# Expert layers with the weight chunks stationary and the tokens moving, and the expert blocks written out

## What is computed

```
logits = t_norm @ router_w + router_b          # 8 experts, the two best taken, weights normalised
gate = x @ gate_w[e] + gate_b[e]               # 256 -> 512
up   = x @ up_w[e] + up_b[e]                   # 256 -> 512
h    = silu(gate) * up
y    = h @ down_w[e] + down_b[e]               # 512 -> 256
t    = t + sum over the two experts of weight * y
```

## Time and profile before

| | us |
|---|---|
| median of 3 runs | 454.25 (454.06 to 455.29) |
| span of the profiled execution | 453.7 |
| first token transposes of the expert blocks to the end of the span | 243.1 to 453.7 |
| busy: PE / DVE / ACT / POOL | 346.5 / 343.3 / 209.2 / 288.8 |
| mean granted TensorE clock | 0.851 |

### The profile page before, as it was taken

One profiled execution on the slowest core, in us unless ns is written; L12 is line 12 of the kernel. 1 busy time (PEld: TensorE's weight loads), 2 busy tenths in 40 slices (PEclk: granted clock), 3 DMA queues, 4 the chain that ended last, 5 costly groups with the idle time before them and its releaser, 6 DMA issues.

```text
span 453.7 us, 13159 instructions
## 1 busy us (share of the span) xinstructions
PE 346.5 (76%) x4491; PEld 214.4 (47%) x4492; DVE 343.3 (76%) x693; ACT 209.2 (46%) x343; POOL 288.8 (64%) x459
## 2 busy tenths in 40 slices
PE   0078677767866766697259998999999999999971
PEld 0077434444444454542023654656566566565540
DVE  6988799799899999877882776666776776677650
ACT  1047637755956857645501433334434434433430
POOL 5616456666666666644585367777877878788651
PEclk9997568668668668689569999999999999999995
DMA  8410002322322222507764132333233333323322
GB/s 197 123 36 1 2 2 96 95 94 97 95 92 92 92 95 94 144 2 194 219 248 139 25 48 46 48 56 58 46 56 55 51 49 55 58 46 58 56 25 23
DMA packets 24960, 35.27 MB, mean 78 GB/s; under 512 B 4992, under 2 KB 18304, under 8 KB 24160
## 3 DMA queue, kind: packets, MB, share of 16 engines
q1 hardware_dynamic: 16256, 24.46, 17.5%
q0 software_dynamic: 7488, 10.23, 14.1%
q10 hardware_dynamic: 1184, 0.14, 0.2%
HBM read 25.39 MB, written 9.44 MB: 77 GB/s over the span
## 4 chain that ended last, share of the span: by engine, by line
PE 25%; DVE 23%; issue 19%; POOL 13%; DMA 9%; ACT 5%; DVEq 2%; POOLq 1%; SPq 1%; ACTq 0%
PE bank L881 6%; DMA w_stage<-token_rows,q_hi 5%; POOL w_stage L513 4%; PE bank L902 3%; POOL small L509 3%; DVE att L1348 2%; PE bank L549 2%; DVE s_exp L1314 2%; DVE v_exp L1367 2%; PE bank L777 2%; DVE q_exp L1382 2%; POOL v_exp L488 2%; PE bank L664 2%; DVE maxes L1307 2%; DMA token_rows<-z_stack 1%
## 5 line engine op out<-in xcount | busy, mean ns | idle before, releaser
L881 PE MATMUL bank<-w_exp,w_stage 128*128 x468 | 113.7, 380 | 1.3 <-issue 0.2
L526 POOL DMA_INDIRECT out_dram<-w_stage,q_hi x39 | 62.4, 1600 | 16.9 <-issue 16.9
L881 PEld LDWEIGHTS bank<-w_exp,w_stage 128*128 128x128 f16 x468 | 45.6, 97 | 41.8 <-issue 4.6
L408 POOL TENSOR_TENSOR w_exp<-w_stage,w_exp 128x1024 f16<-128x1024 f32 (+1 forms) x24 | 51.0, 2129 | 22.4 <-ACT w_exp L1041 22.4
L902 PE MATMUL bank<-w_exp,q_exp 128*128 x468 | 58.6, 276 | 2.1 <-DVE q_exp L1587 2.1
L513 POOL DMA_INDIRECT w_stage<-token_rows,q_hi x39 | 48.1, 1234 | 6.0 <-issue 6.0
L1570 DVE TENSOR_TENSOR v_exp<-bank,x_rows 128x512 f32<-128x512 f32 x39 | 27.0, 692 | 32.9 <-PE bank L881 32.8
L1146 ACT ACTIVATE w_stage<-w_stage,gate 128x256 f32<-128x256 f32 x39 | 19.8, 508 | 68.2 <-DVE w_stage L1592 68.2
L902 PEld LDWEIGHTS bank<-w_exp,q_exp 128*128 128x128 f16 x468 | 43.0, 98 | 11.8 <-issue 5.4
L1127 ACT ACTIVATE w_stage<-bank 128x256 f16<-128x256 f32 x39 | 14.9, 383 | 52.9 <-PE bank L869 52.9
L1587 DVE TENSOR_TENSOR q_exp<-bank,q_exp 128x512 f16<-128x512 f32 x39 | 27.0, 692 | 10.2 <-ACT q_exp L1138 10.0
(11 more groups left out here) (253 smaller groups left out, 814.2 us busy)
## 6 DMA issues: line engine op xcount, KB each, us to landing
w_stage<-in_L_ffn_gate_w_dram SPq DMA_DIRECT2D x8, 512.0 KB, 3.5
w_stage<-in_L_ffn_up_w_dram SPq DMA_DIRECT2D x8, 512.0 KB, 3.5
w_stage<-in_L_ffn_down_w_dram SPq DMA_DIRECT2D x8, 512.0 KB, 3.5
x_rows<-in_x_dram SPq DMA_DIRECT2D x8, 256.0 KB, 6.1
out_dram<-x_rows SPq DMA_DIRECT2D x4, 512.0 KB, 6.0
token_rows<-z_stack SPq DMA_DIRECT2D x4, 512.0 KB, 6.0
x_rows<-in_L_ffn_gate_b_dram SPq DMA_DIRECT2D x1, 2048.0 KB, 11.6
z_stack<-in_L_ffn_up_b_dram SPq DMA_DIRECT2D x2, 1024.0 KB, 6.8
```

The source lines that it names most:

```text
L408: pool.tensor_tensor(lo, w_stage[:, k, :], hi, ALU.subtract).then_inc(s["w_lo_done"], 1)
L526: pool.indirect_dma_start(out, bass.IndirectOffsetOnAxis(s_idx[par], 0), yw[par], None, compute_op=ALU.add).then_inc(s["y_scattered"], 16)
L881: mm = pe.matmul(GU[par][k][:], xs[par][:, c, :], w_exp[:, w * W_EXP + k * W_PIECE + c * FF:][:, bass.ds(e, FF)], start=(n == 0), stop=(n ...
```

## The change

- `hidden` turns its operands round: a 128x128 chunk of the weights is stationary and the 128 tokens move. For each of gate and up there are four chunks f of the 512 FF units, two halves c of the features and three parts: 24 pairs of a weight load and a matmul of 128 columns where there were six of 512. The result has **FF units on partitions**, which is what `down` needs as stationary operand, so `hidden_turned` is gone.
- With FF units on partitions a bias is a column. `gate_b` and `up_b` are loaded once as 64 rows of 128 (`b_rows`), turned by one PE transpose in `fold_vectors` and copied to `b_cols` by DVE. ACT's `silu` reads the gate's PSUM bank and adds the bias itself, in four chunks; DVE's `gated` adds the up bias and multiplies in one instruction a chunk, four a block. The 4 MB of broadcast bias loads and the two bias additions go.
- PE's order is now hidden(b+1, gate), hidden(b+1, up), tokens_in(b+2), down(b). On DVE a block is down_bias(b-1), gated(b+1), tokens_low(b+2), hidden_low(b+1).
- `gather` and `scatter` take the index column of the table directly, without copy; one hold instruction is left, in `scatter`. Gather b+3 stands ahead of scatter b, as in the loop before. The two `xg` buffers stay.
- The loops over blocks are written out in Python on all engines, so block numbers are constants; the expert's number stays in a register.

```diff
@@
-BODY = (BLOCKS - 3) // 4
+FF_CHUNKS = FF // P
...
+        b_cols = sb("b_cols", [P, 2 * EXPERTS * FF // P])
+        b_rows = att_n[0:64, 1, 0:P]
-        gate_b_all = x_rows[:].rearrange("p n l -> p (n l)")
-        up_b_all = xn.rearrange("p n l -> p (n l)")
...
@@ SyncE
+            for i, b in enumerate((gate_b, up_b)):
+                rows = slice(EXPERTS * FF // P * i, EXPERTS * FF // P * (i + 1))
+                sp.dma_start(b_rows[rows, :], b.rearrange("e (f p) -> (e f) p", p=P)).then_inc(s["r_in"], 16)
...
-            sp.wait_ge(s["rt_ps"], 2 * (TILES // 4))
-            sp.dma_start(gate_b_all, gate_b.rearrange("e i -> (e i)").partition_broadcast(P)).then_inc(s["bias_rows"], 16)
...
-                sp.dma_start(up_b_all[:, half], up_rows[half].partition_broadcast(P)).then_inc(s["up_rows"], 16)
@@ GpSimd
-                pool.tensor_copy(g_idx[par], t_gather[:, bass.ds(b, 1)]).then_inc(s["gcol_ready"], 1)
...
+            def gather(b):
+
+                if b >= 2:
                     pool.wait_ge(s["xt_ps"], b - 1)
...
+                pool.indirect_dma_start(xg[b % 2], None, token_rows,
+                                        bass.IndirectOffsetOnAxis(t_gather[:, b:b + 1], 0))\
+                    .then_inc(s[f"x_got{b % 2}"], 16)
+
+            def scatter(b):
+
+                pool.wait_ge(s["y_ready"], b + 1)
+                if b >= 1:
                     pool.wait_ge(s["y_scattered"], 16 * b)
...
+                pool.tensor_tensor(hold[b], one_word, one_word, ALU.mult)
+                pool.indirect_dma_start(out, bass.IndirectOffsetOnAxis(t_scatter[:, b:b + 1], 0), yw[b % 2], None,
...
+            for b in range(3):
+                gather(b)
+            for b in range(BLOCKS):
+                if b + 3 < BLOCKS:
+                    gather(b + 3)
+                scatter(b)
@@ TensorE
-                pe.wait_ge(s["r_in"], 32)
+                pe.wait_ge(s["r_in"], 64)
+                pe.transpose(bank[7][:, 256:256 + 2 * EXPERTS * FF // P], b_rows, ident[0:64, 0:64])
...
+            def hidden(b, k, e):
 
                 if k == 0:
                     pe.wait_ge(s["xl_ready"], b + 1)
...
+                if b >= 2:
+                    pe.wait_ge(s["silu_ready"] if k == 0 else s["h_ready"], FF_CHUNKS * (b - 1))
+                for f in range(FF_CHUNKS):
                     for c in range(2):
...
+                        for xs, w in ((x_hi, 0), (x_lo, 0), (x_hi, 1)):
+                            mm = pe.matmul(GU[b % 2][k][:, P * f:P * f + P],
+                                           w_exp[:, w * W_EXP + k * W_PIECE + c * FF + P * f:][:, bass.ds(e, P)],
+                                           xs[b % 2][:, c, :], start=(c == 0 and xs is x_hi and w == 0),
+                                           stop=(c == 1 and w == 1))
+                mm.then_inc(s["gate_ps"] if k == 0 else s["up_ps"], 1)
...
-                    mm = pe.transpose(HT[:, P * c:P * c + P], h_sb[par][:, P * c:P * c + P], ident[:])
...
+            for b in range(BLOCKS):
+                if b + 1 < BLOCKS:
+                    e = weights_of(b + 1)
+                    hidden(b + 1, 0, e)
+                    hidden(b + 1, 1, e)
+                e = weights_of(b)
+                if b + 2 < BLOCKS:
+                    load_expert(b + 2)
+                    tokens_in(b + 2)
+                down(b, e)
@@ ScalarE
+            def silu(b):
+                e = act.value_load(t_expert[0:1, b:b + 1], min_val=0, max_val=EXPERTS - 1)
...
+                act.wait_ge(s["gate_ps"], b + 1)
+                for f in range(FF_CHUNKS):
+                    act.activation(g_silu[b % 2][:, P * f:P * f + P], bank[2 * (b % 2)][:, P * f:P * f + P], ACT.Silu,
+                                   bias=b_cols[:, bass.ds(e * FF_CHUNKS + f, 1)]).then_inc(s["silu_ready"], 1)
...
+            for b in range(BLOCKS):
+                if b >= 1:
+                    weigh(b - 1)
+                if b + 1 < BLOCKS:
+                    silu(b + 1)
+                if b + 2 < BLOCKS:
+                    tokens_high(b + 2)
+                if b + 1 < BLOCKS:
+                    hidden_high(b + 1)
+            weigh(BLOCKS - 1)
@@ VectorE
+                    step(dve.tensor_copy(b_cols[:], bank[7][:, 256:256 + 2 * EXPERTS * FF // P]))
...
+            def gated(b):
+                e = expert_of(b)
...
+                dve.wait_ge(s["up_ps"], b + 1)
+                for f in range(FF_CHUNKS):
+                    cols = slice(P * f, P * f + P)
+                    dve.wait_ge(s["silu_ready"], FF_CHUNKS * b + f + 1)
+                    dve.scalar_tensor_tensor(
+                        out=h_sb[b % 2][:, cols], in0=bank[2 * (b % 2) + 1][:, cols],
+                        scalar=b_cols[:, bass.ds(e * FF_CHUNKS + EXPERTS * FF_CHUNKS + f, 1)],
+                        in1=g_silu[b % 2][:, cols], op0=ALU.add, op1=ALU.mult).then_inc(s["h_ready"], 1)
...
+            for b in range(BLOCKS):
+                if b >= 1:
+                    down_bias(b - 1)
+                if b + 1 < BLOCKS:
+                    gated(b + 1)
+                if b + 2 < BLOCKS:
+                    tokens_low(b + 2)
+                if b + 1 < BLOCKS:
+                    hidden_low(b + 1)
+            down_bias(BLOCKS - 1)
```

More of the change, by code:

```diff
@@ L496, in _ @@
             pool.wait_ge(s["pad_out"], 16)
[L500 to L505, removed]
+            hold = [ga_flat[0:1, 256 + i:257 + i] for i in range(BLOCKS)]
+            one_word = t_weight[0:1, 0:1]
+            def gather(b):
+                if b >= 2:
                     pool.wait_ge(s["xt_ps"], b - 1)
-                    pool.wait_ge(s[f"x_got{par}"], 16 * turn)
-                    pool.wait_ge(s["gcol_ready"], b)
-                    pool.tensor_tensor(hold[0], one_word, one_word, ALU.mult)
-                pool.tensor_copy(g_idx[par], t_gather[:, bass.ds(b, 1)]).then_inc(s["gcol_ready"], 1)
[L511 to L514, removed]
@@ L896, in down @@
+            def down(b, e):
                 pe.wait_ge(s["hl_ready"], b + 1)
-                if not first:
+                if b >= 1:
                     pe.wait_ge(s["yadd_ready"], b)
                 n = 0
-                for c in range(4):
+                for c in range(FF_CHUNKS):
                     for hs, w in ((h_hi, 0), (h_lo, 0), (h_hi, 1)):
-                        mm = pe.matmul(YB[:, 0:L_COL], hs[par][:, c, :],
+                        mm = pe.matmul(YB[:, 0:L_COL], hs[b % 2][:, c, :],
@@ L1608, in _ @@
-            tokens_low(0, 0)
-            tokens_low(1, 1)
-            e0 = expert_of(0)
-            dve.wait_ge(s["bias_rows"], 32)
-            gate_bias(0, 0, e0, first=True)
-            dve.wait_ge(s["up_rows"], 32)
-            up_bias(0, 0, e0)
-            gated(0, 0, first=True)
-            dve_block(0, 0, first=True)
-            with dve.Fori(0, BODY) as i:
-                for k in range(4):
-                    dve_block(4 * i + k + 1, (k + 1) % 2)
-            dve_block(BLOCKS - 2, 1, more=1)
@@ L1621, in _ @@
-            dve_block(BLOCKS - 1, 0, more=0)
+            tokens_low(0)
+            gated(0)
+            tokens_low(1)
+            hidden_low(0)
+            dve.wait_ge(s["bias_rows"], 16)
+            for b in range(BLOCKS):
+                if b >= 1:
+                    down_bias(b - 1)
[5 more added lines that the diff above has]
+                    hidden_low(b + 1)
```

211 lines of the change are left out of this document (53 added, 158 removed).

## The result

| | before | after |
|---|---|---|
| median | 454.22 us (454.06 to 455.29, 4 runs) | 506.26 us (505.67 to 506.65, 4 runs) |
| span of the profiled execution | 453.7 | 504.6 |
| ratio of the runs | | 1.115 (95% interval 1.112 to 1.118) |
| mean granted TensorE clock | 0.851 | 0.867 |

A forecast was written before the change was run, and what follows sets the result against it. PE's register steps, in a loop closing through DVE, were to bound each block: up(1) ends at 255.05, plus 37 periods of 6.05 us, 17.25 of tail, 0.25 for the bias copy and 0.55 around the span: 497.0 us, range 484 to 524.

The forecast's parts named there:

- 0.125 us a step: PE's queue: each register-addressed weight slice costs a 0.125 us step; gate and up's 32 take 4.0 us a block.
- A loop that closes through DVE: From up's end through hand-off, four DVE chunks, tokens_low and PE's 31 further steps: 6.05 us a block against 4.94.
- The overlap beside it: PE's queue: register load, token transposes and down's 8 steps, 1.5 us, fit into the 1.95 us PE waits.
- the hand-off does not close: Rival: DVE's chunks don't delay the tokens, PE's queue alone needs 5.6 us a block, 480 us; chance 0.04.
- Beside the loop and buy nothing: Removed hidden transposes (0.43 us of PE), bias additions and old product (2.1 us of DVE) gain nothing.
- "nothing" for GpSimd: Dropping index copies and three of four hold instructions on GpSimd was priced at nothing.
- The floor of 4.4 us for the scatters: GpSimd: each scatter waits for the previous landing; 3.8 us, 0.18 hold and some 0.4 issue give 4.4 us.
- The clock: Rival: PE's clock falls to 1.2 GHz, a block takes 7.3 us; 521 us with half the blocks; chance 0.18.
- Not the bound: Rival: in gate and up an idle PE is fed every 0.057 us, block 4.85 us, 450.2 us; chance 0.06.
- dearer loads: Rival: every register-addressed weight load costs a step, 48 instead of 32, block 8.05 us, 571 us; chance 0.05.
- the first rival: Gate and up steps stay but PE's queue feeds pairs every 0.057 us, 450.2 us; chance 0.06.
- The start: Before the blocks: copying the turned bias on DVE adds 0.25 us; 0.55 us lies around the profiled span.

The follow-up runs named there:

- e1: Changed kernel with PE taking expert b mod 8 as a constant, so no register steps on PE: 449.59 us, ratio to before 0.991.
- e9: Changed kernel with up's weights at a constant address and gate's by the register, 16 of hidden's 32 register steps left: 477.33 us, ratio 1.051.
- e5: Kernel before with each 512-column gate and up matmul cut into four of 128 columns, tokens still stationary, 32 register steps: 511.53 us, ratio 1.125.
- e10: Changed kernel with token transposes between gate and up on PE, tokens_high ahead of silu, tokens_low ahead of the gated chunks: 507.09 us, ratio 1.117.
- e7: Kernel before with only blocks written out and the change's gather and scatter on GpSimd, without index copies: 445.20 us, ratio 0.981.
- e3: Changed kernel without high tokens times low weights in gate and up, 32 pairs and 16 register steps a block: 451.72 us, ratio 0.994.
- e2: Changed kernel without low tokens times high weights in gate and up, 32 pairs but still 32 register steps a block: 505.29 us, ratio 1.113.
- e4: Changed kernel with tokens_low(b+2) ahead of gated(b+1) on DVE, all else alike: 506.22 us, ratio 1.115.

## Why the prediction was right, and where not

- **Direction and mechanism: right, and shown.** 32 register steps a block for slices that had been 8. Without them the changed kernel runs in 449.6 us (e1), with half of them in 477.3 (e9), and the old operand order gets as slow when it is given as many steps (e5).
- **0.125 us a step: low by 0.007.** The single spacing is right (in the trace of the changed kernel 87% of the gaps between hidden's steps are 0.124 to 0.125 us); the others are longer, and 31 gaps fill 4.1 us, 0.132 each. 31 x 0.007 = 0.2 us a block is the difference between the 6.05 of the sum and the 6.26 measured, and 37 times that, 7.7 us, most of the 9.3 us by which the forecast was low. This is the term that was mis-sized.
- **"A loop that closes through DVE": the step that failed.** Its length was right by two misses that cancel: `tokens_low` starts 1.04 us after the first chunk where the sum had 1.28 (timeline of DVE below), and the hand-off is 0.33 in place of 0.11, with DVE's own queue instructions ahead of the first chunk. But it isn't what sets the pace: without it a block of PE alone still takes 6.19 us (e10). The overlap beside it was wrong too, that the rest of PE's queue would fit into the 1.95 us that it waits: priced at 1.5 us, it takes 1.9 and more and fills the wait. The loop does set the pace once there are half as many steps (e9).

```profile
344.04 1.13 DVE L1528 SCALAR_TENSOR_TENSOR w_stage<-bank,b_cols,v_exp 128x128 f32<-128x128 f32 x4 [3.09 <-PE bank L852]
345.08 0.41 DVE L1513 TENSOR_TENSOR w_stage<-bank,w_stage 128x256 f16<-128x256 f32 x1
```

- **The rival "the hand-off does not close" (5.6 us, 480) named the right chain at the wrong price.** It counted 40 steps and the register load. In the queue of one block above, 6.3 us lie between two register loads: 40 x 0.132 = 5.3 are steps, 0.3 is the load, and the other 0.7 are the two MOVEs and three semaphores with the gaps around them, which had no price.
- **"Beside the loop and buy nothing": right here, as PE's queue covers it all,** but "nothing" for GpSimd was true only under that cover. Alone it is worth 9.5 us (e7), which the change throws away. The floor of 4.4 us for the scatters was too low: where e3 has one scatter waiting for the landing of the other they are 4.70 us apart, 3.87 to the landing, 0.14 to the hold and 0.69 from the hold to the scatter.
- **The clock: right to hold it the smaller case.** It stays at 1.00 at 6.25 us a block.
- **"Not the bound", "dearer loads": both out.** e1 shows 0.057 us a pair without steps, e2 that a load without a step of its own costs nothing. That e1's 449.6 us lies beside the 450.2 of the first rival is no point for it: there the steps are gone, and the rival had them in place and hidden.
- **The start**: PE's first token transposes come 0.7 us later than before (243.81 for 243.1), where the sum had 0.25; and 1.66 us lie around the span of 504.6, where it took 0.55. The 0.55 compared a span with the median of other runs; taken run by run, the kernel before too is some 1.8 us longer than its span (454.38 and 452.6, for one).

```profile
243.81 0.38 PE L840 MATMUL bank<-ident,w_stage 128*128 128x128 f32 x2
```

## What to carry to other kernels

On TensorE an address that is known only at run time cost an instruction in the engine's own queue for each different slice, and no busy share showed it; count them for a block (0.13 us each here, and semaphores, moves and register loads with them) and compare with what the array has to stream meanwhile. On TensorE, cut what has a run-time address into as few and as long slices as possible, whichever operand it is: 12 matmuls of 512 columns hid 8 steps, 48 of 128 columns were starved by 32. And when a bundle of edits is slower, run its parts alone: here one was worth 2%.

## What the runs showed of the hardware that I had not expected

- A register step on TensorE takes 46 ns by the profile, but the next one starts 0.124 us later, with one or two matmuls between them; a matmul without a step follows after 0.057 us, load included. Removing 16 pairs that share another's step changed the time by 0.2%.
- Three paths of nearly the same length lie side by side in these kernels: PE's queue (6.19 us in e10), the loop through DVE (6.26 us at most, in the changed kernel), and the loop of ACT and DVE in e4 (6.2 us). An edit that takes one away and lengthens another leaves the time within 0.2%, so read the chain of the edited kernel before drawing on its time.
- GpSimd's own small instructions could set the pace of the kernel before: with index copies, holds and a loop its row took 4.93 us a block. In e7, without them, a gather takes 1.00 us in place of 1.46, and a scatter starts 0.34 us after its hold in place of 0.97.
